# Score and value products issued in four parts, with a quarter of a projection or of transpositions behind each part

## The reference

```python
def attn_layer(x, Wqkv, qs, ksc, Wo):                 # 16 heads of 64, INNER = 1024
    q, k, v = jnp.split(x @ Wqkv, 3, -1)              # then split into heads
    q = l2norm(q) * qs
    k = l2norm(k) * ksc
    q = q * cos * scale + rotate_half(q) * sin * scale
    k = k * cos * inv + rotate_half(k) * sin * inv
    out = local_attention(q, k, v)                    # windows of 32 tokens, each looks at itself
    return out @ Wo                                   # and at the 32 tokens before it
def local_attention(q, k, v):
    sim = jnp.einsum('bhwie,bhwje->bhwij', bq, bk2) * QK_SCALE     # 32 x 64 per window and head
    attn = jax.nn.softmax(jnp.where(mask, -jnp.finfo(sim.dtype).max, sim), -1)
    out = jnp.einsum('bhwij,bhwje->bhwie', attn, bv2)
def ffn_layer(x, g, bln, W1, b1, W2, b2):
    return a * jax.nn.gelu(gate, approximate=False) @ W2 + b2      # a, gate from layernorm(x) @ W1
```

## Time and profile before

| | |
|---|---|
| median of three runs | 5213.91 us |
| profiled execution, its device time | 5238.39 us |
| its span, first to last instruction | 5236.6 us |
| PE busy | 4141.3 us, 79% of the span |
| DVE busy | 3477.7 us, 66% |
| ACT busy | 3135.9 us, 60% |
| POOL busy | 1083.3 us, 21% |
| mean granted TensorE clock | 0.926 of full speed |

### The profile page before, as it was taken

One profiled execution on the slowest core, in us unless ns is written; L12 is line 12 of the kernel. 1 busy time (PEld: TensorE's weight loads), 2 busy tenths in 40 slices (PEclk: granted clock), 3 DMA queues, 4 the chain that ended last, 5 costly groups with the idle time before them and its releaser, 6 DMA issues. The chain is left out here.

```text
span 5236.6 us, 176300 instructions
## 1 busy us (share of the span) xinstructions
PE 4141.3 (79%) x68250; PEld 2934.0 (56%) x68250; DVE 3477.7 (66%) x6841; ACT 3135.9 (60%) x8480; POOL 1083.3 (21%) x856
## 2 busy tenths in 40 slices
PE   5665588888888888888888888888888888885368
PEld 4443466666666666665666566666666666653134
DVE  4444577767777677666777676767776777764655
ACT  2332366766666666666666676767666767662123
POOL 0000222222222222222222222222222222220012
PEclk8776799999999999999999999999999999996579
DMA  0001233333333333333333333333333333320000
GB/s 25 0 0 39 58 78 74 74 76 85 86 74 73 75 81 88 78 75 75 81 84 78 75 75 74 89 80 74 74 75 87 84 74 76 76 67 11 0 9 12
DMA packets 138442, 336.61 MB, mean 64 GB/s; under 512 B 44880, under 2 KB 46032, under 8 KB 137552
## 3 DMA queue, kind: packets, MB, share of 16 engines
q1 hardware_dynamic: 137808, 326.67, 26.5%
HBM read 22.41 MB, written 2.10 MB: 5 GB/s over the span
## 5 line engine op out<-in xcount | busy, mean ns | idle before, releaser
L990 ACT ACTIVATE loc_probs<-loc_pair,loc_ebias,loc_rnorm 128x64 f32<-128x64 f32 x3072 | 1199.5, 430 | 14.1 <-DVE loc_ebias L1150 11.7
L691 POOL TENSOR_TENSOR loc_ks<-loc_mcos,loc_swapped 128x1024 f32<-128x1024 f32 x192 | 453.3, 2361 | 1854.7 <-DVE loc_kr L1138 1363.1
L738 PE MATMUL loc_pair<-loc_hs,loc_wqk 128*128 128x256 f32 x3072 | 763.4, 392 | 40.5 <-issue 36.3
L990 ACT ACTIVATION_READ_ACCUMULATOR loc_probs<-loc_pair,loc_ebias,loc_rnorm 128x1 f32 x3072 | 710.2, 231 | 0.0
L691 POOL TENSOR_TENSOR loc_qr<-loc_mcos,loc_swapped 128x1024 f32<-128x1024 f32 x192 | 452.9, 2359 | 1210.1 <-DMA loc_swapped<-loc_msin 1210.1
L738 PEld LDWEIGHTS loc_pair<-loc_hs,loc_wqk 128*128 128x128 f32 x3072 | 572.7, 194 | 149.8 <-issue 55.0
L1090 DVE SCALAR_TENSOR_TENSOR loc_mcos<-loc_pair,loc_scal,loc_tab 128x1024 f32<-128x1024 f32 x384 | 490.9, 1278 | 197.0 <-ACT loc_sq L972 178.6
L1148 DVE TENSOR_REDUCE loc_mx<-loc_pair 128x8 f32<-128x512 f32 x384 | 264.4, 688 | 480.4 <-PE loc_pair L782 472.4
L972 ACT ACTIVATE loc_sq<-loc_pair 128x1024 f32<-128x1024 f32 x384 | 395.8, 1031 | 276.1 <-PE loc_pair L738 276.0
L1099 DVE SCALAR_TENSOR_TENSOR loc_msin<-loc_pair,loc_scal,loc_tab 128x1024 f32<-128x1024 f32 x384 | 489.9, 1276 | 33.7 <-DMA loc_swapped<-loc_msin 33.4
L782 PE MATMUL loc_pair<-loc_kr,loc_qr 64*32 64x64 f32 x24576 | 321.9, 227 | 151.8 <-issue 151.7
(11 more groups left out here) (244 smaller groups left out, 7419.5 us busy)
## 6 DMA issues: line engine op xcount, KB each, us to landing
loc_swapped<-loc_msin SPq DMA_DIRECT2D x1536, 128.0 KB, 2.3
loc_veven<-loc_vodd SPq DMA_DIRECT2D x768, 64.0 KB, 2.0
loc_veven<-loc_vodd SPq DMA_DIRECT2D x384, 128.0 KB, 2.3
loc_wqk<-wqk_dram SPq DMA_DIRECT2D x12, 512.0 KB, 3.7
loc_wv<-wv_dram SPq DMA_DIRECT2D x6, 512.0 KB, 3.3
loc_wo<-wo_dram SPq DMA_DIRECT2D x6, 512.0 KB, 4.4
x<-xT_dram SPq DMA_DIRECT2D x1, 2048.0 KB, 7.5
loc_tab<-tables_dram SPq DMA_DIRECT2D x1, 2048.0 KB, 7.7
```

Source lines behind the costliest of these rows:

```text
L691: nc.gpsimd.tensor_tensor(dst, mcos[i % 2][:, :], swapped[:, :], ALU.add).then_inc(rope_add, 1)
L738: ins = nc.tensor.matmul(pairs[b][:, p // 2, (p % 2) * UNIT:(p % 2 + 1) * UNIT], wqk[:, k, w:w + P], hs[u.odd][:, :], start=True, stop=True)
L990: ins = nc.scalar.activation(probs[x][:, p, hp, :], pairs[b][:, hp, p * 2 * WIN:(p + 1) * 2 * WIN], ACT.Exp, bias=ebias[x][:, k:k + 1], sc ...
```

## The change

Four pairs of calls, one after the other in `step`, become interleaved calls. `scores` and `weighted` get an argument `beside`, a function, and call it after each quarter of their small products (after every second of the eight pairs of heads). `project`, `spread` and `outputs_across` get an argument `quarters` and issue only those quarters of their work.

| before, in this order | after |
|---|---|
| `project(2)`, then `weighted(1)` | `weighted(1)` in four parts, a quarter of `project(2)` behind each |
| `scores(1)`, then `project(3)` | `scores(1)` in four parts, a quarter of `project(3)` behind each |
| `spread(0)`, then `weighted(0)` | `weighted(0)` in four parts, a quarter of `spread(0)` behind each |
| `scores(0)`, then `outputs_across(0)` | `scores(0)` in four parts, a quarter of `outputs_across(0)` behind each |

The number of products, their shapes and their operands stay as they are. The `vacated` waits of both calls of a pair now stand ahead of the pair. The semaphore of the small products is raised behind their last part, that of the other call behind its last quarter.

```diff
-            def spread(x, u, b):
-                if u is None:
-                    return
-                after(pe, wide_ready, u.n, 2, x + 1)
-                for p in range(PAIRS):
+            def spread(x, u, b, quarters=range(4)):
+                if u is None:
+                    return
+                if 0 in quarters:
+                    after(pe, wide_ready, u.n, 2, x + 1)
+                for p in range(2 * quarters[0], 2 * quarters[-1] + 2):
                     ins = nc.tensor.transpose(pairs[b][:, p // 4, (p % 4) * BLK:(p % 4 + 1) * BLK], rk_wide[:, p * P:(p + 1) * P], ident[:, :])
-                ins.then_inc(spread_ps, 1)
-
-            def scores(x, u, b):
-                if u is None:
+                if 3 in quarters:
+                    ins.then_inc(spread_ps, 1)
+
+            def scores(x, u, b, beside):
+
+                if u is None:
+                    for quarter in range(4):
+                        beside([quarter])
                     return
...
-                ins.then_inc(sim_ps, 1)
+                    if p == PAIRS - 1:
+                        ins.then_inc(sim_ps, 1)
+                    if p % 2:
+                        beside([p // 2])
...
             def step(at):
                 if at(2) is not None:
                     vacated(pe, ((oT_ready, at(4), 2, 1), (kr_ready, at(3), 2, 1),))
-                    project(2, at(2), 2)
                 if at(4) is not None:
                     vacated(pe, ((kr_ready, at(3), 2, 2), (v_ready, at(4), 2, 2),))
-                    weighted(1, at(4), 0)
+                weighted(1, at(4), 0, lambda quarter: project(2, at(2), 2, quarter))
...
-                    scores(1, at(3), 2)
                 if at(2) is not None:
                     vacated(pe, ((oT_ready, at(4), 2, 2), (exp_ready, at(3), 4, 2), (rot, at(2), 8, 2),))
-                    project(3, at(2), 1)
+                scores(1, at(3), 2, lambda quarter: project(3, at(2), 1, quarter))
...
-                    spread(0, at(2), 2)
                 if at(3) is not None:
                     vacated(pe, ((rot, at(1), 8, 2), (rot, at(2), 8, 8), (oT_ready, at(4), 2, 2),))
-                    weighted(0, at(3), 1)
+                weighted(0, at(3), 1, lambda quarter: spread(0, at(2), 2, quarter))
...
-                    scores(0, at(2), 1)
                 if at(3) is not None:
                     vacated(pe, ((probsT_ready, at(3), 2, 2),))
-                    outputs_across(0, at(3), 2)
+                scores(0, at(2), 1, lambda quarter: outputs_across(0, at(3), 2, quarter))
```

31 lines of the change are left out of this document (20 added, 11 removed).

## The result

The changed kernel is slower: 5897.47 us median of 4 runs (5890.4 to 5915.64) against 5214.32 us (5198.06 to 5218.83), a ratio of 1.1323 with a 95% interval of 1.1299 to 1.1348. The direction is as forecast and the size is not: +683 us where +262 was forecast, and outside the range.

The account below looks back on a forecast made before the run. PE's instruction stops and the chain between engines bound the kernel. Five items gave 46.1 us a step against 43.37, +2.7 over 96 steps, +262 us: 5500 profiled, 5476 median; range 5280 to 5640, the forecast's own 5390 to 5580.

Parts of the forecast that it names:

- Item 4: From `norms` to the end of `rotate_sin(0)`, untouched by the change: 12.62 us in one step, 11.12 in the other.
- What bounds the kernel: PE's stops in runs of small products, apparently late instructions, 248 us; and the chain of waits between PE, DVE and ACT.
- The price of a change: PE switching between small and large products: 0.33 us a round trip with a projection, 0.29 with transpositions, 3.7 a step.
- quarters in under 0.9 us: Sign of being wrong: score quarters following each other faster than this mean the price of a change is too high.
- Item 1: `weighted(1)` with `project(2)`: waits for `scale_keys(1)`, block lasts 4.4 us, to 5.85 after `ln_mean`; later square costed at nothing.
- Item 2: From `ln_var` to the mask of `scores(1)`: PE nearly gapless, 6.80 us, so the mask is at 12.65.
- Item 3: `scores(1)` with `project(3)`: last scores +2.43 us, `norms` at 22.8; the removed 2.21 us stop pays in the long step only.
- Item 5: Step's end: `spread(0)` and `weighted(0)` wait for `rotate_sin(0)`, then the mask of `scores(0)` for ACT's copy; 11.9 us in all.
- The stops go, 248 us of them: PE's stops in small products vanish, from 248 us to under 60, but later ends fill their places.
- the stops stay: Rival, chance 0.12: PE's instructions stay late, perhaps in blocks with transpositions; 0.5 to all of 248 us on top, 5600 to 5720.
- Stops inside the quarters: Sign of being wrong: PE still stopping within the quarters of small products.
- steadier work: Granted clock, 0.96 in the long step against 0.99 in the short, may gain a little more; argued for the faster case.

Follow-up runs that it names:

- in one part: The change's order and pooled waits against the kernel before, each run of 64 small products whole, then all the other work, no interleaving: 5824.26 us, 1.1206.
- all_waits: The kernel before in its old order, but in all four pairs every wait of both calls stands ahead of the pair: 5467.73 us, 1.0518.

## Why the prediction was wrong

Starts of PE's groups in 91 steps of each trace, averaged (this table is worked out from the timelines; us per segment):

```
                              before  forecast  after   in one part
ln_mean -> ln_var               5.32    5.85     7.53      8.08
ln_var -> mask of scores(1)     7.51    6.80     8.49      8.39
mask -> norms                   7.98   10.15     9.10      8.12
norms -> third pair            11.62   11.5     12.45     12.24
third pair -> step's end       10.98   11.9     12.89     12.57
```

- **In the terms of the sum.** The forecast of +2.7 us a step was +3.7 for round trips, -2.6 for the stops, nothing for the clock, and so +1.6 for later ends. Measured are +1.8, -0.8, +1.5 and +4.4. Three terms were short by 6.1 us, and the price of the round trips was too high by 1.9, which by luck hid part of it: with that price right, the forecast would have been under +1 us. Item 4 has a slip besides: 22.8 + 12.62 is 35.4, not 34.7, so the step's end should have reached 47.3.
- **What bounds the kernel.** Right on both counts: stops of PE's instruction supply, and the chain between engines. But I took the stops as something to be removed, and didn't ask where the edges of blocks would lie in the new order.
- **The price of a change, 3.7 us a step.** Right that both directions cost time, wrong in size: 0.15 to 0.2 us a round trip in place of 0.33 and 0.29, so 1.8 to 2.4 us a step. As the prediction put it, quarters in under 0.9 us would show the price too high: those with transpositions follow in 0.75, those with a projection in 1.02 (1.1 forecast). The Trainium skill's rule in "TensorEngine Tiling (Array Packing)", Key Properties, that a change of mode drains the engine, agrees with a price, and these rows give its size.
- **Item 1, `weighted(1)` with `project(2)`: the step that failed most.** Forecast were 5.85 us, +0.5 over the average before, with no stop in it and at full clock. Measured are 7.53. Stops in `weighted(1)` take 1.12 us of that, before 0.16, and the lower clock up to 0.75. The runs on this pair show why: the projection had been the cover under which the next block of instructions arrived. With the pair turned round PE stops after 28 products, and the half clock behind the stop stretches the projection from 1.99 to 2.97 us. The prediction had such stops before it in the earlier trace rows, but didn't ask which other runs they could land in. The later square of `project(2)` it costed at nothing; ACT's 512 us of waiting for projections in place of 276 speak against that, but how much of it reached the step's end isn't shown.
- **Item 2.** "Nearly gapless, 6.80 us" was the length in one short step; the average before is 7.51, so 0.7 us of the base were missing. Another 1.0 came on top, and it is waits: PE's for DVE's `loc_rstd` and ACT's `loc_h` rose from 0.1 to 1.2 us a step. So the stretch that was called gapless is where the late end of item 1 was paid for again; why `loc_rstd` comes so much later wasn't tried.
- **Item 3.** Mask to `norms` grew by 1.12 us, not 2.2: the round trips are cheaper, and the removed stop pays here as said (0.92 to 0.16 us a step in `scores(1)`). PE's wait for DVE's gate rose from 0.96 to 2.36 us, which the forecast had in its sum.
- **Item 4.** "Which the change doesn't touch" grew by 0.83 us, with no instruction moved. It is where the lower clock shows: `norms` products at 464 ns for 386. At clock 1.00 a group of 32 takes 1.93 us in either kernel, but in the changed one 31 of 75 groups, each behind PE's wait for the gate, run partly at the lower clock.
- **Item 5, the step's end.** The waits are the ones that were named, in that order, and in the good step it takes 11.15 us (2923.90 to 2935.05). On average it is 1.0 us over the 11.9 forecast, with 0.8 us of stops and up to 0.9 of lower clock in it.
- **"The stops go, 248 us of them".** Wrong. In scores and value products 153.5 + 40.5 = 194 us are left, in shorter and more frequent pieces, where under 60 was the mark. The rival "the stops stay", at 0.12, was right that they do, but looked for them in the blocks with transpositions. More than half of what is left is in `weighted(1)`, between the quarters of a projection: 1.12 of 2.1 us a step. Stops inside the quarters were named as a sign of being wrong. Its price of 5600 to 5720 us counted the stops alone.
- **The clock.** Between 700 and 4500 us the mean granted clock is, in the last three columns of the view of stretches (clock, DMA share, GB/s), first before, then after:

```profile
700.00:4500.00 3800.00, 3230.51 (x60356) 2341.20 (x60362) 2699.01 (x5170) 2614.87 (x7362) 931.05 (x700) 0.98 0.34 78
```

```profile
700.00:4500.00 3800.00, 3039.16 (x51938) 1952.95 (x51927) 2473.55 (x4453) 2256.38 (x6341) 799.80 (x601) 0.95 0.29 67
```

The levels are 0.5 and 1.0, and the trace has 386 of the 3800 us at the lower one, before 181. That is 5.2 us a step for 2.1, and if everything took twice as long in it, 1.5 us a step were lost by the change, some 150 us in all: an estimate, since no run held the clock fixed. The forecast expected steadier work and had the clock at nothing.

The waits alone (`all_waits`, some +270 us) cost as much as the forecast gave for everything. What stays open: stops, lower clock and waits bring each other about, so the table says where PE's time goes and not what it would be without one of them; and why the four pairs cost 2.8 points more together than apart. Also, the place of the edges alone moved the kernel before by -2.15% to +0.44% and the changed one by up to 2.9 points. So a difference of up to about 3 points between two of these kernels can't be put down to the edit with certainty: that holds for one, two or four parts, for the waits or the order of one pair, and for the 2.8 points. That the change loses is safe. At the three positions at which both kernels were run (none, 64 and 192 instructions ahead) it costs 13.2, 11.7 and 12.8% of the kernel before at the same position. That the waits and the order each cost something is likely too, at 5.2 and 6.9%, but their sizes rest on one position each.

## What to carry to other kernels

Where engines take turns, an order that makes one of them finish each piece later is paid for at every turn: here PE's waits for the others grew by 4.4 of the 7.0 us that a step lost, and waits pooled ahead of two calls cost alone as much as everything that the forecast had counted. Large products between runs of small ones are not idle time to be tidied: in this kernel late instructions arrived under them, so before reordering, count the instructions of each run, and look in the trace when the next packet of the instruction queue comes. And before a difference of a per cent or two is put down to an edit of a kernel with many small instructions, shift the unchanged kernel by half a block and see what that does.

## What the runs showed of the hardware

- Where the instructions lie is worth per cents: 64, 128 and 192 instructions ahead of the loop gave 1.0020, 1.0044 and 0.9785 of the same kernel, and took the changed one from 1.1323 to 1.1189 (64) and 1.1033 (192).
- In runs of 64x64 products that use 256 instructions in 1.5 us PE stopped, mostly for 1.4 to 2.2 us, and all 126 of the stops of 1 us or more in the kernel before ended 1.1 to 1.6 us after a packet of 16,384 bytes on the instruction queue.
- Behind such stops, and twice as often in the changed kernel behind PE's waits for other engines (67 of 100 falls), the granted clock fell: to 0.50 over 2 us at 2740, and with the first pair turned round, eight products of the projection took 2.97 us in place of 1.99.
- One change from 64x64 products to large ones and back costs PE 0.15 to 0.2 us, with a projection (quarters 1.02 us apart for 0.85 of work) or with transpositions (0.75 for 0.60).
